# Two pairs of banks for the first batch's row maxima, and later slots for projection, gate and expert choice

## The chip, the cores and the metric

The kernel runs on one core of one Trainium2 chip. The metric is the device time of one execution in microseconds. The engines of the core run side by side, each through its own list of instructions in order, and meet only at semaphores: TensorE (PE, with its weight loads as PEld), VectorE (DVE), ScalarE (ACT), GpSimd (POOL), and SyncE (SP), which issues DMAs.

## The reference, cut to what matters

Eight sequences of 256 token ids go through one block of a language model with width 256:

```python
h = onehot(x) @ embeddings                           # (8, 256, 256)
qkv = layernorm(h) @ w_qkv                           # 16 heads of 16
q, k = rotary(q), rotary(k)
attn = softmax(q @ k.T * 16**-0.5)                   # (8, 16, 256, 256)
h = h + (attn @ v) @ w_proj
y = layernorm(h)
chosen = argmax(y @ gate_w.T)                        # one of 8 experts for each token
h = h + (y + (y @ expert_w[chosen].T))
```

Everything is float32. The kernel splits each float32 operand of a product into a high part that fits TensorE's fast format and a low remainder, and adds up three products (high by high, low by high, high by low), so each projection is three matmuls for each half of the width.

## The kernel before, in words

One batch is one sequence: 256 tokens, two tiles `t` of 128 rows. The work is a pipeline over batches, written out by hand. `step(b)` has 16 slots `s`; in it each engine works on several batches at once. In even slots TensorE does `visit(b, v)` with `v = s // 2`: for two heads it makes the transposed scores T of batch b (`t_scores_tile`, into `t_pair`, two banks of PSUM), which ScalarE turns into probabilities with `exp`, and the scores S of batch b+1 (`scores_tile`, into `s_pair`, two more banks), of which VectorE takes the row maxima with `maximum`. A matmul for S waits until `maximum` has read what its bank held before. The maxima are split into two parts (`max_split`), turned by TensorE into rows (`first_max_transpose` for the first half of batch 0, otherwise `max_transpose`), copied by ScalarE (`max_row`) and written by a DMA into the stack of operands, so that T comes out with its maximum already subtracted.

Beside the visits, tables give each remaining piece of work a slot. `FRONT`, `EARLY`, `TWO` and `FOUR` are for the front of batch k (normalise, transpose x, project q and k, rotate, transpose, project v); batch 2 has the table `TWO`, and the part of its front that is not in the table is written out ahead of step 0. `POST` is for what follows the attention of batch k and is counted from slot 0 of step k+1: `o0`, `o1` (transposes of the outputs), `on`, `o_low`, `proj` (`out_project`), `residual`, `stats`, `g_norm`, `y`, `y_low`, `gate`, `gate_t`, `choose`. The experts of batch b-2 run in step b, one unit of six matmuls in every even slot (`experts`), and VectorE adds each unit, masked by the choice, to `acc` (`select`). Up to step 6 all units write the one bank `e_bank`, so unit n waits until `select` of unit n-1 has read it. The loop `for s in range(SLOTS)` in each engine's `step` fixes in what order the pieces of one slot are issued.

GpSimd adds the two halves of the rotation (`rotated_sum`), takes the inverse square roots, gathers the embedding rows of batch b+4 in slot 1 of step b (two indirect DMAs, `gather`), and in slots 1, 5, 9 and 13 of steps 0 and 1 makes the low parts of the expert weights (`expert_weights`).

Ahead of step 0 stands an opening that is written out: the fronts of batches 0, 1 and in part 2, and the eight visits `visit(-1, v)` that make only S of batch 0. `fill` issues matmuls with a result that nothing reads. `first_restack` on SP moves batch 1's operands by DMA into their stack, and step 0 starts with batch 1's S and batch 0's T.

Of the kernel before, what the change touches and what calls it, by code (L numbers as in the profile page):

```python
# [35 lines left out]
def tower(nc, x, emb, w_qkv, w_proj, gate_w, expert_w, rope, ramp, out):  # L36
# [12 lines left out]
    with ExitStack() as ctx:  # L49
# [76 lines left out]
        def pair_of_banks(name):  # L126
# [47 lines left out]

        FRONT = dict(stats=-8, norm=-6, x=-5, x_low=-4, qk0=-3, qk1=-1, rotate0=-2, rotate1=0, t0=1, low0=2, t1=3, low1=4, v=5)
        EARLY = dict(stats=-12, norm=-9, x=-7, x_low=-6, qk0=-5, qk1=-4, rotate0=-3, rotate1=-2, t0=0, low0=1, t1=2, low1=3, v=5)
        TWO = dict(rotate0=0, rotate1=1, t0=2, low0=3, t1=4, low1=5, v=7)
        FOUR = dict(FRONT, stats=-10, norm=-8, x=-7, x_low=-6, qk0=-5, rotate0=-3, qk1=-2)
        POST = dict(o0=2, o1=4, norm0=3, norm1=5, on=6, o_low=7, proj=8, residual=9, stats=10, g_norm=11,
                    y=12, y_low=13, gate=14, gate_t=15, choose=15)  # L180
        LAST = dict(o0=2, o1=2, norm0=3, norm1=3, on=4, o_low=5, proj=6, residual=7, stats=7, g_norm=8,
                    y=9, y_low=10, gate=11, gate_t=12, choose=12)

# [51 lines left out]

        def maxima_slot(b):

            return 10 if b < 3 else 11

        def place(h):  # L240

# [115 lines left out]
        def _(pool):  # L357
# [19 lines left out]
            def f_rs_of(b):  # L377
# [3 lines left out]
                wait(pool, f_var, b + 1)  # L381
                g.tensor_tensor(f_rs[:, :], f_ve[:, :], neg_half[:, :], ALU.pow).then_inc(f_rstd, 1)

            def rotated_sum(b, t):
                wait(pool, roped, b * 2 * NT + 2 * t + 2)
                if b == 1:
                    pool.wait_ge(z_hi, 2 * t + 2)
                    pool.wait_ge(z_dup_q, t + 1)
                    pool.wait_ge(z_dup_k, t + 1)
                    pool.wait_ge(z_lo, 2 * t + 2)  # L390

                j = 4 if b == 1 else 8
                turned = qk[:, t, :, :, :].rearrange("p g d j -> p (g d j)").rearrange("p (g d j) -> p g j d", d=HD, j=j)
                g.tensor_tensor(turned, rope_a[:, t, :, :].rearrange("p (g j) d -> p g j d", j=j),  # L394
                                rope_b[:, t, :, :].rearrange("p (g j) d -> p g j d", j=j),
                                ALU.add).then_inc(rotated, 1)
# [60 lines left out]
            rotated_sum(1, 0)  # L457
            rotated_sum(1, 1)
            f_rs_of(2)
            gather(3)  # L460
            gate_weights()
            proj_weights_low()
# [4 lines left out]
        def _(pe):  # L467
# [44 lines left out]
            def project_qk(b, t, parts=range(C)):  # L512
                if parts[0] > 0:
                    pass
                elif t == 0:
                    if b == 0:
                        pe.wait_ge(wqkv_l_ok, C)
                    wait(pe, xl_ok, b + 1)
                    if b == 2:
                        wait(pe, qkl_ok, 1)  # L520
                elif b == 2:
                    wait(pe, qkl_ok, 2)
                elif b == 3:
                    wait(pe, qkl_ok, (b - 1) * NT)
                elif b > 3:
                    wait(pe, roped, b * 2 * NT + 2)
                x_h, x_l = x_parts(b)
                m = product(front_bank(b, t)[:, :], lambda c: x_h[:, c, t, :], lambda c: x_l[:, c, t, :],
                            lambda c: wqkv_h[:, c, 0:2 * D], lambda c: wqkv_l[:, c, 0:2 * D], parts)
                if parts[-1] == C - 1:  # L530
                    m.then_inc(qk_ps, 1)
# [33 lines left out]
            def scores_wait(b, v, half):  # L565
                if b == 0 and v == 0:
                    wait(pe, z_in, z_copied(1, 1))
                elif b == 0 and v in (4, 6):
                    wait(pe, z_in, max(z_copied(0, v // 2), z_copied(1, v // 2)))
                elif b == 1 and v % 4 == 0:  # L570
                    wait(pe, half_in[v // 4], 96)
                elif v == 0:
                    wait(pe, stack_in, (b - 2) * 96 + 96)
                wait(pe, max_ok, b * NH + 2 * v - half)

            def scores_tile(b, v, half, t):
                r, pair = place(2 * v + half)
                m = mm(s_pair[:, half, t * N:(t + 1) * N], stacks[b % STACKS][r:r + KS, pair, 0, t * P:(t + 1) * P],  # L578
                       stacks[b % STACKS][r:r + KS, pair, 1, :], start=True, stop=True)
                if t == NT - 1:  # L580
                    m.then_inc(s_ps, 1)

            def first_max_transpose():

                pe.wait_ge(roped, 2 * 2 * NT)
                pe.wait_ge(ml_ok, 1)
                for t in range(NT):
                    m = tr(t_bank[1][0:16, N + t * P:N + (t + 1) * P].bitcast(F32R),
                           max_parts[:, 0, t, :, :, :].rearrange("p i a j -> p (i a j)"), ident_r[:, :])
                m.then_inc(mt_ps, 1)  # L590

# [11 lines left out]
            def t_scores_wait(b, v, half):  # L603
                if v == 0 and b == 1:
                    pe.wait_ge(ones_in, 64)
                if v == 0 and b == 0:
                    pe.wait_ge(wp_l_ok, 1)
                    pe.wait_ge(gw_l_ok, 1)
                    pe.wait_ge(roped, 2 * 2 * NT)
                    pe.wait_ge(filled, VALS + 1)  # L610
                if v % 4 == 0:
                    wait(pe, m_in[v // 4], b * 32 + 32)
                wait(pe, exp_ok, b * NH + 2 * v + half - 1)

            def t_scores_tile(b, v, half, c):
# [108 lines left out]
            def step(b, p):  # L724
                for s in range(SLOTS):
                    g_at = SLOTS * b + s
                    if s % 2 == 0:
                        visit(b, s // 2)
                        if b == 0 and s == 0:
                            project_qk(2, 1, [1])  # L730
                            pe.wait_ge(xl_ok, 3)
                        if b == 0:
                            fill(m_bank, 3 if s == 0 else 4 if s == 2 else 1)
                    if here(b, 0) and s == 3:
                        max_transpose(b, 1)
                    if here(b, 1) and s == maxima_slot(b + 1):
# [53 lines left out]
            z_transpose(1)  # L790
            visit(-1, 0)
            qk_transpose(1, 0)
            visit(-1, 1)
            qk_transpose(1, 1)
            visit(-1, 2)
            x_transpose(2)
            visit(-1, 3)
            project_v(0, [0])
            first_max_transpose()
            visit(-1, 4)  # L800
            project_v(0, [1])
            project_qk(2, 0, [0])
            visit(-1, 5)
            project_v(1, [0])
            project_qk(2, 0, [1])
            visit(-1, 6)
            project_v(1, [1])
            visit(-1, 7)
            project_qk(2, 1, [0])
            steps(step)  # L810


        @block.scalar
        def _(act):
# [35 lines left out]

            def max_row(b, u):
                wait(act, mt_ps, b * 2 + u + 1)
                turned = t_bank[1] if b == 0 and u == 0 else o_bank
                copy(max_rows[:, u, :], turned[0:16, N:2 * N]).then_inc(mt_ok, 1)
                if b == 0 and u == 0:
                    act.wait_ge(mt_ok, 1)
                    for half in range(2):
                        r = 64 * half + KS
                        act.dma_start(stacks[0][r:r + 2, 0:4, 0, :].bitcast(F32),
                                      max_rows[8 * half:8 * half + 8, u, :].bitcast(F32)).then_inc(m_in[u], 16)  # L860
# [77 lines left out]
                z_copy(t, q)  # L938
            qk_high(1, 0)
            qk_high(1, 1)  # L940
            qk_high_again(1, 0)
            qk_high_again(1, 1)
            x_high(2)
            max_row(0, 0)
            values(0)
            values(1)
            steps(step)


# [1 line left out]
        def _(dve):  # L951
# [48 lines left out]
            def maximum(b, k):  # L1000
                for half in (1, 0):
                    wait(dve, s_ps, b * NH + 2 * k + 2 - half)
                    v.tensor_reduce(neg_max[:, k // 4, :, 4 * half + k % 4],  # L1003
                                    s_pair[:, half, :].rearrange("p (t n) -> p t n", t=NT), AX.X, ALU.max,
                                    negate=True).then_inc(max_ok, 1)

            def max_split(b, u):
# [115 lines left out]
            def step(b, p):  # L1123
                for s in range(SLOTS):
# [9 lines left out]
                            g_norm_a(k)  # L1134
                    for k in batches(post, "g_norm", g_at):
                        g_norm_b(k)
                    if here(b, -2) and s > 0 and unit_in(b, s - 1) is not None:
                        select(b - 2, p, unit_in(b, s - 1), expert_banks(b - 2))
                    for k in batches(front, "stats", g_at):
# [19 lines left out]
                            g_norm_a(k)  # L1159
                    for k in batches(post, "y_low", g_at):  # L1160
                        y_low(k, k % 2)
                    for k in batches(post, "choose", g_at):
                        choose(k, k % 2)

            dve.sem_inc(acc_ok, 1)
            for b in range(NB):
                v.memset(h0[:, b * NT:(b + 1) * NT, :], 0.0).then_inc(h_zero, 1)
# [26 lines left out]
                v.memset(vals[i][:, :, :, HD:HD + 1], 1.0).then_inc(filled, 1)  # L1194
            maximum(0, 0)
            f_norm_a(2)
            maximum(0, 1)
            f_norm_b(2)
            qk_low(1, 0)
            maximum(0, 2)  # L1200
            qk_low(1, 1)
            maximum(0, 3)
            max_split(0, 0)
            x_low(2)
# [32 lines left out]
```

## Time and profile before

| | us |
|---|---|
| median of 3 runs | 310.89 (310.54 to 310.95) |
| profiled execution, its own time | 310.0 |
| its span | 308.2 |
| PE busy | 283.4 (92% of the span) |
| DVE busy | 243.4 (79%) |
| ACT busy | 132.7 (43%) |
| POOL busy | 85.9 (28%) |
| mean granted TensorE clock | 0.983 of full |

The span runs from the first to the last instruction, and the execution's own time is 1.8 us more. A busy time is the sum of the records of an engine; matmul records overlap, so a full PE share does not say that the PE does all it could. The page gives the PE 64% of the chain of work that ended last, and DVE 24%.

### The profile page before, as it was taken

To read this page: it belongs to the slowest core of one execution; us is meant where nothing else is said; L and a number is where in the kernel's file an instruction comes from. 1 tells how busy PE (TensorE), PEld (TensorE's weight loads), DVE (VectorE), ACT (ScalarE), POOL (GpSimd) and SP (SyncE) were. 2 spreads that over 40 slices of the span, in tenths; PEclk is the share of its full clock that TensorE was granted. 3 is DMA by queue.
4 is the path that set the end of the run, shared out by engine and by line. 5 is a ranking of instruction groups with operands and counts; after the bars stand their busy time and mean duration, and the time that the engine had idled before them with its cause. 6 is when DMAs were issued, how large, how long until landed. Compare 5 with 4: busy or idle time off the path is not lost.

```text
span 308.2 us, 5639 instructions
## 1 busy us (share of the span) xinstructions
PE 283.4 (92%) x2063; PEld 203.1 (66%) x2063; DVE 243.4 (79%) x602; ACT 132.7 (43%) x271; POOL 85.9 (28%) x103
## 2 busy tenths in 40 slices
PE   2998799888879999999999999999999999999895
PEld 2775566656646776777767776777666666667674
DVE  8798569968987799887988698878898874656765
ACT  3166117748664534364426433453453444331000
POOL 5736305636265012431222033201200210210300
PEclk9999579999999999999999999999999999999999
DMA  4530410830930580039101940166010010000011
GB/s 117 182 149 17 160 45 6 167 49 14 161 47 5 95 120 2 0 93 147 17 2 36 147 60 2 36 116 94 2 37 1 4 36 2 1 12 26 0 36 34
DMA packets 10803, 17.55 MB, mean 57 GB/s; under 512 B 2024, under 2 KB 4883, under 8 KB 10648
## 3 DMA queue, kind: packets, MB, share of 16 engines
q1 hardware_dynamic: 9988, 16.62, 26.2%
q0 software_dynamic: 768, 0.55, 0.7%
q8 instruction: 17, 0.28, 0.4%
q14 instruction: 10, 0.08, 0.1%
q10 hardware_dynamic: 20, 0.02, 0.0%
HBM read 5.30 MB, written 2.10 MB: 24 GB/s over the span
## 4 chain that ended last, share of the span: by engine, by line
PE 64%; DVE 24%; ACT 5%; issue 3%; DMA 1%; POOL 0%; SPq 0%; DVEq 0%; ACTq 0%
PE e_bank L475 18%; PE f_bank L475 10%; PE o_bank L652 9%; DVE neg_max L1003 7%; PE t_pair L617 5%; DVE acc L1101 4%; PE s_pair L475 4%; PE s_pair L578 3%; PE m_bank L475 3%; PE s_pair L481 2%; PE o_bank L475 2%; PE m_bank L666 2%; PE m_bank L698 2%; ACT probs L867 2%; ACT parts L816 1%
## 5 line engine op out<-in xcount | busy, mean ns | idle before, releaser
L867 ACT ACTIVATE probs<-t_pair 128x512 f32<-128x512 f32 x128 | 69.5, 595 | 80.1 <-PE t_pair L617 79.6
L1003 DVE TENSOR_REDUCE neg_max<-s_pair 128x2 f32<-128x512 f32 x128 | 81.9, 682 | 13.0 <-PE s_pair L578 12.8
L578 PE MATMUL s_pair<-stacks 48*128 48x256 f32 x256 | 49.5, 316 | 1.5 <-DVE neg_max L1003 0.8
L617 PEld LDWEIGHTS t_pair<-stacks 50*128 50x128 f32 x256 | 32.8, 186 | 22.7 <-issue 20.8
L617 PE MATMUL t_pair<-stacks 50*128 50x256 f32 x256 | 46.6, 308 | 1.1 <-DVE neg_max L1003 0.6
L475 PE MATMUL e_bank<-ew_h,y_h 128*128 128x512 f32 x92 | 40.3, 438 | 1.9 <-DVE acc L1101 1.5
L1101 DVE SCALAR_TENSOR_TENSOR acc<-e_bank,mask,acc 128x256 f32<-128x256 f32 x66 | 28.8, 478 | 11.8 <-PE e_bank L475 11.7
L578 PEld LDWEIGHTS s_pair<-stacks 48*128 48x128 f32 x256 | 34.3, 190 | 4.5 <-DVE neg_max L1003 3.5
L475 PE MATMUL e_bank<-ew_l,y_h 128*128 128x512 f32 x92 | 36.4, 396 | 0.0
L394 POOL TENSOR_TENSOR qk<-rope_a,rope_b 128x512 f32<-128x512 f32 x16 | 20.8, 1301 | 56.2 <-DVE rope_b L990 56.2
L475 PE MATMUL e_bank<-ew_h,y_l 128*128 128x512 f32 x92 | 36.2, 394 | 0.0
L652 PE MATMUL o_bank<-probs,vals 128*32 128x256 f32 x512 | 34.2, 385 | 0.0
L475 PEld LDWEIGHTS e_bank<-ew_h,y_h 128*128 128x128 f32 x92 | 17.3, 188 | 8.9 <-DVE acc L1101 3.9
L652 PEld LDWEIGHTS o_bank<-probs,vals 128*32 128x32 f32 x512 | 13.4, 109 | 12.2 <-issue 5.0
L400 POOL TENSOR_SCALAR g_ve<-g_mv 128x2 f32<-128x2 f32 x8 | 1.9, 243 | 68.9 <-DVE g_mv L959 68.9
L475 PEld LDWEIGHTS e_bank<-ew_l,y_h 128*128 128x128 f32 x92 | 17.3, 188 | 4.1
L370 POOL DMA_INDIRECT h<-in_emb,ids x16 | 17.6, 1098 | 5.5 <-issue 3.3
L816 ACT ACTIVATE o_t<-o_bank 128x256 f32<-128x256 f32 x32 | 12.5, 389 | 14.7 <-PE o_bank L652 14.7
L475 PEld LDWEIGHTS e_bank<-ew_h,y_l 128*128 128x128 f32 x92 | 17.4, 189 | 2.1
L475 PE MATMUL f_bank<-wqkv_h,x_h 128*128 128x256 f32 (+1 forms) x46 | 16.5, 358 | 1.8 <-DVE x_l L974 1.8
L475 PE MATMUL f_bank<-wqkv_h,x_l 128*128 128x256 f32 (+1 forms) x46 | 15.7, 342 | 0.0
L475 PE MATMUL f_bank<-wqkv_l,x_h 128*128 128x256 f32 (+1 forms) x46 | 15.7, 341 | 0.0
(177 smaller groups left out, 542.5 us busy)
## 6 DMA issues: line engine op xcount, KB each, us to landing
stacks<-parts SPq DMA_DIRECT2D x36, 256.0 KB, 6.7
ew_raw<-in_expert_w SPq DMA_DIRECT2D x1, 2048.0 KB, 8.5
out<-res SPq DMA_DIRECT2D x7, 256.0 KB, 2.1
stacks<-parts SPq DMA_DIRECT2D x12, 128.0 KB, 2.8
probs<-in_w_qkv SPq DMA_DIRECT2D x2, 384.0 KB, 3.8
stacks<-max_rows SPq DMA_DIRECT2D x30, 8.0 KB
h<-in_emb,ids POOLq DMA_INDIRECT x16, 2.7
probs<-in_w_proj SPq DMA_DIRECT2D x1, 256.0 KB, 2.7
```

The lines of the kernel that those rows point to most:

```text
L370: g.indirect_dma_start(h0[:, j, :], None, emb, bass.IndirectOffsetOnAxis(ap=ids[:, j:j + 1], axis=0), bounds_check=V - 1, oob_is_err=False ...
L394: g.tensor_tensor(turned, rope_a[:, t, :, :].rearrange("p (g j) d -> p g j d", j=j), rope_b[:, t, :, :].rearrange("p (g j) d -> p g j d", ...
L475: m = mm(o, a(c), w(c), start=(c == 0 and n == 0), stop=(c == C - 1 and n == 2))
L481: mm(o[:, :], wqkv_h[:, 0, 0:P], wqkv_h[:, 0, 0:512], start=True, stop=True)
L578: m = mm(s_pair[:, half, t * N:(t + 1) * N], stacks[b % STACKS][r:r + KS, pair, 0, t * P:(t + 1) * P], stacks[b % STACKS][r:r + KS, pair, ...
L617: m = mm(t_pair[:, half, c * N:(c + 1) * N], stacks[b % STACKS][r:r + KM, pair, 1, c * P:(c + 1) * P], stacks[b % STACKS][r:r + KM, pair, ...
L652: m = mm(o_bank[STRIP * j:STRIP * (j + 1), 0:N], vals[b % VALS][:, c, head(4 * g + j), :], probs[:, (4 * g + j) % RING, c, :], start=(c == ...
L666: m = tr(strips_bank(b, t)[:, g * P:(g + 1) * P], o_t[:, g, t * P:(t + 1) * P], ident[:, :])
L816: return nc.scalar.activation(o, i, ACT.Copy)
L867: nc.scalar.activation(probs[:, (2 * v + half) % RING, :, :].rearrange("p c n -> p (c n)"), t_pair[:, half, :], ACT.Exp, scale=SCALE).then ...
L1003: v.tensor_reduce(neg_max[:, k // 4, :, 4 * half + k % 4], s_pair[:, half, :].rearrange("p (t n) -> p t n", t=NT), AX.X, ALU.max, negate=T ...
L1101: v.scalar_tensor_tensor(out=acc[:, j, t, :], in0=y, scalar=mask[:, p, t, e:e + 1], in1=base[:, t, :] if u == 0 else acc[:, j, t, :], op0= ...
```

## The change

Batch 0's S visits with odd `v` go to `t_pair`, which batch 0's T does not need yet; their waits on `max_ok` are those of the visit before last, and the first T waits for all 16 maxima. The order of the opening on TensorE, ScalarE and VectorE is rearranged, with five fills in it; the last third of batch 2's projection moves from slot 0 of step 0 into it; and the normalisation of batch 2 goes from VectorE (`f_norm_b(2)`) to GpSimd (`normed(2)`). In `TWO` the rotations of batch 2 go from slots 0 and 1 to 1 and 3, its transposes and low parts one slot later. In `POST`, `proj` goes from slot 8 to 9, `gate` from 14 to 15, `gate_t` from 15 to 16 and `choose` from 15 to 17; `residual` stays at 9. `choose` is now issued ahead of `select` within a slot. `maxima_slot` is 11 for every batch.

```diff
-        TWO = dict(rotate0=0, rotate1=1, t0=2, low0=3, t1=4, low1=5, v=7)
+        TWO = dict(rotate0=1, rotate1=3, t0=3, low0=4, t1=5, low1=6, v=7)
-        POST = dict(o0=2, o1=4, norm0=3, norm1=5, on=6, o_low=7, proj=8, residual=9, stats=10, g_norm=11,
-                    y=12, y_low=13, gate=14, gate_t=15, choose=15)
+        POST = dict(o0=2, o1=4, norm0=3, norm1=5, on=6, o_low=7, proj=9, residual=9, stats=10, g_norm=11,
+                    y=12, y_low=13, gate=15, gate_t=16, choose=17)
...
         def maxima_slot(b):
-            return 10 if b < 3 else 11
+            return 11
+
+        def scores_pair(b, v):
+            return t_pair if b == 0 and v % 2 else s_pair
...
+            def normed(b):
+                pool.wait_ge(f_rstd, b + 1)
+                for t in range(NT):
+                    g.tensor_scalar(xn[:, t, :], h0[:, b * NT + t, :], f_mv[:, t, 0:1], f_rs[:, t:t + 1],
+                                    ALU.subtract, ALU.mult).then_inc(f_normed, 1)
...
             f_rs_of(2)
+            normed(2)
             gather(3)
...
                 elif v == 0:
                     wait(pe, stack_in, (b - 2) * 96 + 96)
-                wait(pe, max_ok, b * NH + 2 * v - half)
+                if b == 0 and v == 1:
+                    pe.wait_ge(roped, 2 * 2 * NT)
+                if b == 0:
+                    wait(pe, max_ok, 2 * v - 2 - half if v > 1 else 0)
+                else:
+                    wait(pe, max_ok, b * NH + 2 * v - half)
...
+                if v == 0 and b == 0:
+                    pe.wait_ge(max_ok, NH)
                 wait(pe, exp_ok, b * NH + 2 * v + half - 1)
...
                         visit(b, s // 2)
-                        if b == 0 and s == 0:
-                            project_qk(2, 1, [1])
-                            pe.wait_ge(xl_ok, 3)
                         if b == 0:
-                            fill(m_bank, 3 if s == 0 else 4 if s == 2 else 1)
+                            fill(m_bank, 3 if s < 4 else 1)
...
             z_transpose(1)
             visit(-1, 0)
             qk_transpose(1, 0)
+            project_v(0, [0])
             visit(-1, 1)
             qk_transpose(1, 1)
+            project_v(0, [1])
             visit(-1, 2)
+            fill(m_bank, 1)
+            project_v(1, [0])
+            visit(-1, 3)
             x_transpose(2)
-            visit(-1, 3)
-            project_v(0, [0])
+            project_v(1, [1])
+            visit(-1, 4)
             first_max_transpose()
-            visit(-1, 4)
-            project_v(0, [1])
             project_qk(2, 0, [0])
             visit(-1, 5)
-            project_v(1, [0])
             project_qk(2, 0, [1])
+            fill(m_bank, 1)
             visit(-1, 6)
-            project_v(1, [1])
+            project_qk(2, 1, [0])
+            fill(m_bank, 1)
             visit(-1, 7)
-            project_qk(2, 1, [0])
+            project_qk(2, 1, [1])
+            fill(m_bank, 2)
             steps(step)
...
             qk_high(1, 0)
             qk_high(1, 1)
+            values(0)
             qk_high_again(1, 0)
             qk_high_again(1, 1)
             x_high(2)
+            values(1)
             max_row(0, 0)
-            values(0)
-            values(1)
...
             maximum(0, 0)
             f_norm_a(2)
+            qk_low(1, 0)
             maximum(0, 1)
-            f_norm_b(2)
-            qk_low(1, 0)
+            qk_low(1, 1)
             maximum(0, 2)
-            qk_low(1, 1)
             maximum(0, 3)
```

Left out of the diff are `first_max_transpose` and `max_row`, which use `e_bank` in place of a bank of `t_pair` for batch 0's first turn, with the waits that belong to it, and VectorE's `maximum`, which reads `scores_pair(b, k)`.

## Rows read from the trace of the kernel before

**Rows 1.** The page: the granted clock of TensorE in 40 slices.

```profile
PEclk9999579999999999999999999999999999999999
```

**Rows 2.** Windows: the opening and steps 0, 3 and 5; busy us, clock, DMA share.

```profile
25.40:46.10 20.70, 17.52 (x79) 12.18 (x79) 13.85 (x29) 6.12 (x12) 5.78 (x7) 0.75 0.25 82
46.10:68.70 22.60, 20.68 (x169) 13.85 (x169) 19.26 (x37) 14.96 (x30) 11.20 (x11) 1.00 0.42 75
...
127.50:160.50 33.00, 32.18 (x251) 23.50 (x250) 28.30 (x74) 14.69 (x31) 9.35 (x11) 1.00 0.35 61
...
193.50:222.70 29.20, 28.52 (x235) 20.89 (x234) 23.62 (x55) 14.35 (x30) 4.92 (x6) 1.00 0.37 65
```

**Rows 3.** Windows of one us of PE alone: length, PE busy, clock, DMA share, GB/s.

```profile
31.00:32.00 1.00, 0.58 (x3) 0.93 0.63 186
...
42.00:43.00 1.00, 1.00 (x7) 0.95 0.00 0
```

**Rows 4.** Timeline of PE, the first fills: start, us, instruction.

```profile
5.71 5.84 PE L481 MATMUL s_pair<-wqkv_h 128*128 128x512 f32 x13 [5.71 <-ACT wqkv_h L816]
...
11.74 1.41 PE L481 MATMUL s_pair<-wqkv_h 128*128 128x512 f32 x5
```

**Rows 5.** Timeline of DVE, the opening and step 0.

```profile
25.99 1.29 DVE L1003 TENSOR_REDUCE neg_max<-s_pair 128x2 f32<-128x512 f32 x2 [0.52 <-PE s_pair L578]
...
28.07 1.26 DVE L1003 TENSOR_REDUCE neg_max<-s_pair 128x2 f32<-128x512 f32 x2
...
29.99 0.67 DVE L995 TENSOR_TENSOR parts<-f_bank,parts 128x512 fp32r<-128x512 f32 x1
...
56.35 1.18 DVE L1010 CAST max_parts<-neg_max 128x16 fp32r<-128x16 f32 x1
```

**Rows 6.** Chain of waits, opening and step 1: start, us, engine, tile, line, count.

```profile
22.51 1.46 PE t_pair L475 x6
...
25.45 0.56 PE s_pair L578 x4
...
38.38 1.65 PE f_bank L475 x3
...
75.80 1.43 PE f_bank L475 x12
```

**Rows 7.** Timeline of ACT, the last copy ahead of `project_v(0, [0])`.

```profile
26.71 0.65 ACT L816 ACTIVATE stacks<-o_bank 128x512 fp32r<-128x512 f32 x1
```

**Rows 8.** Timeline of POOL in step 0.

```profile
50.18 1.29 POOL L394 TENSOR_TENSOR qk<-rope_a,rope_b 128x512 f32<-128x512 f32 x1 [1.08 <-DVE rope_b L990]
51.61 1.02 POOL L370 DMA_INDIRECT h<-in_emb,ids  x1
52.93 1.00 POOL L370 DMA_INDIRECT h<-in_emb,ids  x1 [0.30 <-issue]
53.96 1.29 POOL L417 TENSOR_TENSOR ew_l<-ew_raw,ew_h 128x512 fp32r<-128x512 f32 x1
55.21 0.22 POOL L380 TENSOR_SCALAR f_ve<-f_mv 128x2 f32<-128x2 f32 x1
```

**Rows 9.** Chain of waits in step 3.

```profile
139.09 1.00 PE o_bank L652 x16
...
147.09 0.67 DVE h L1033 x2
...
151.54 0.48 DVE acc L1101
...
152.06 1.66 PE e_bank L475 x6
```

**Rows 10.** Timeline of PE: waits in step 1, in step 2 and near the end.

```profile
91.69 0.29 PE L698 MATMUL m_bank<-y_h,gw_parts 128*16 128x256 f32 x1 [0.70 <-DVE y_l L1048]
...
96.62 0.66 PE L545 MATMUL f_bank<-ident,qk 128*128 128x128 f32 x4 [0.38 <-DVE rope_b L990]
...
293.22 0.29 PE L706 MATMUL m_bank<-ident,gate_rows 16*128 16x16 f32 x2 [0.46 <-ACT gate_rows L816]
```

More of the change, by code:

```diff
@@ L521, in project_qk @@
                 elif b == 2:
-                    wait(pe, qkl_ok, 2)
+                    wait(pe, mt_ok, 1)
                 elif b == 3:
@@ L573, in scores_wait @@
                     wait(pe, stack_in, (b - 2) * 96 + 96)
-                wait(pe, max_ok, b * NH + 2 * v - half)
+                if b == 0 and v == 1:
[4 more added lines that the diff above has]
+                    wait(pe, max_ok, b * NH + 2 * v - half)
             def scores_tile(b, v, half, t):
                 r, pair = place(2 * v + half)
-                m = mm(s_pair[:, half, t * N:(t + 1) * N], stacks[b % STACKS][r:r + KS, pair, 0, t * P:(t + 1) * P],
+                m = mm(scores_pair(b, v)[:, half, t * N:(t + 1) * N], stacks[b % STACKS][r:r + KS, pair, 0, t * P:(t + 1) * P],
                        stacks[b % STACKS][r:r + KS, pair, 1, :], start=True, stop=True)
@@ L583, in first_max_transpose @@
             def first_max_transpose():
-                pe.wait_ge(roped, 2 * 2 * NT)
+                pe.wait_ge(qkl_ok, NT)
                 pe.wait_ge(ml_ok, 1)
                 for t in range(NT):
-                    m = tr(t_bank[1][0:16, N + t * P:N + (t + 1) * P].bitcast(F32R),
+                    m = tr(e_bank[0:16, N + t * P:N + (t + 1) * P].bitcast(F32R),
                            max_parts[:, 0, t, :, :, :].rearrange("p i a j -> p (i a j)"), ident_r[:, :])
@@ L852, in max_row @@
                 wait(act, mt_ps, b * 2 + u + 1)
-                turned = t_bank[1] if b == 0 and u == 0 else o_bank
+                turned = e_bank if b == 0 and u == 0 else o_bank
                 copy(max_rows[:, u, :], turned[0:16, N:2 * N]).then_inc(mt_ok, 1)
@@ L1003, in maximum @@
                     v.tensor_reduce(neg_max[:, k // 4, :, 4 * half + k % 4],
-                                    s_pair[:, half, :].rearrange("p (t n) -> p t n", t=NT), AX.X, ALU.max,
+                                    scores_pair(b, k)[:, half, :].rearrange("p (t n) -> p t n", t=NT), AX.X, ALU.max,
                                     negate=True).then_inc(max_ok, 1)
@@ L1136, in step @@
                         g_norm_b(k)
+                    for k in batches(post, "choose", g_at):
+                        choose(k, k % 2)
                     if here(b, -2) and s > 0 and unit_in(b, s - 1) is not None:
@@ L1161, in step @@
                         y_low(k, k % 2)
-                    for k in batches(post, "choose", g_at):
-                        choose(k, k % 2)
             dve.sem_inc(acc_ok, 1)
```

## The prediction

> **What bounds the kernel now.** I read the slices of the page first: the granted clock is full everywhere except in slices 4 to 6 [rows 1]. The windows by step then show three regimes. The opening from the first visit takes 20.7 us at a mean clock of 0.75 [rows 2], and windows of one us bound its slow stretch: the clock falls just before 32 and is back just after 42, so 10.2 us at 1.2 GHz in place of 2.4 [rows 3]. Ahead of the fall the PE had thin work: visits, transposes, and waits for `maximum`, 0.58 busy in the last microsecond. In step 0 both PE and DVE are nearly full. In steps 3 and 5 the PE is busy for 32.2 of 33.0 and 28.5 of 29.2 us [rows 2]: what delays the PE there is paid in full. The chain of step 3 shows where DVE holds it: from the residual of `proj` at 147.09 DVE works almost without a pause to a `select` that ends at 152.02, and the next expert unit starts at 152.06 [rows 9].
>
> **The opening.** Four facts give the new one. (a) Prices at full clock: six 512-column matmuls 1.46, so 0.73 for three; six 256-column ones 0.72, half of twelve at 1.43; an S visit 0.5 to its next neighbour, 0.56 to the maximum [rows 6]; a fill 0.28 with its tail, 0.24 in a row [rows 4]. At half clock three 512-column ones took 1.65 [rows 6]. (b) `project_v(0, [0])` waits for ScalarE's last stack copy, until 27.36 [rows 7]. (c) DVE takes 1.2 from one maximum to the next start, 0.88 for the statistics (27.19 to 28.07), 0.6 for a low part [rows 5]. (d) A visit no longer waits for the maximum directly before it.
>
> I put TensorE's new list in order with these: products of v from 27.4, visit 1 at 28.2, transposes, products, visit 2 at 30.0, a fill, products, visit 3 at 31.55, x transposes, products, visit 4 at 33.35, then the turn of the maxima (it waits for DVE's split, done at 33.55) and four groups of three 512-column matmuls with visits 5, 6, 7 between, the last visit at 38.1. DVE reads the last maxima from 38.55 to 39.8. Step 0 starts at 39.9 in place of 46.1: **minus 6.2**. DVE alone would allow 38.7; if the clock fell again as before, the PE list at half price gives 43.9. I take 39.9, because the PE is idle for only 1.0 us (26.4 to 27.4) and then issues without a gap, unlike before the old fall. The DMAs of `first_restack` were issued after the low parts; these end earlier now, so the data should be there.
>
> POOL's `normed(2)` is not in the trace. The nearest rows are 1.29 for two 512-wide inputs and 0.22 for two columns [rows 8]; so 0.4 to 2.6 for both halves, I take 1.5. It is done at 30.8, the x transposes want it at 32.05; only the upper end reaches them. It also moves `gather(3)` and POOL's low projection weights 1.5 later, close to DVE's `max_split`. The trace shows what such a meeting costs: the cast of 56.35 took 1.18 [rows 5] while POOL made expert weights, so 1.0 lost. I price it at zero with 1.0 as its upper end. The Trainium skill ("SBUF — State Buffer", section "SBUF: two separate sides") says why and would make it order-dependent: whichever of a two-input or fast-mode VectorE operation and a GpSimd operation starts first holds their shared port for the whole instruction. By that page the opening loses 1.0 only if POOL comes first, and the sum would be 1.0 higher.
>
> **Step 0, the queue of POOL.** This is the part that goes wrong. Times from the start of the step: the visit, DVE's first maximum from 0.57 to 1.8, then `rotate(2, 0)`, two operations of 0.6, to 3.05 (before, it ran ahead of the maximum). POOL's sum takes 1.29, so `qk_transpose(2, 0)` is issued at 4.5. The PE has by 3.1 done visit 1, three fills and the turn, and waits 1.4. The second half is worse. In slot 1 of POOL `gather(4)` and `expert_weights([0])` stand behind `rotated_sum(2, 0)`, and `rotated_sum(2, 1)` is now in slot 3, behind them. In the trace both sums came first; from the end of the second, at 51.47, two gathers and one weight part went until 55.21, 3.74 us [rows 8]. So the second sum runs from 4.42 + 3.74 = 8.17 to 9.46, and `qk_transpose(2, 1)`, its outputs and all that follow wait until 9.5, after visit 2 has ended at about 5.8: 3.7 us of idle PE. From there I count transposes 0.45, outputs 1.0, visit and fill 0.9, `project_v(2)` 1.45, visit and fill 0.9, x transposes 0.45, outputs 1.0: visit 5 at 15.65. Before, it stood at 13.96, with 1.0 of that the cast above. **Plus 1.7.** Bounds: minus 1.0 (POOL not in the way) and plus 2.7 (the cast held again). From visit 5 on the order is the old one: `maxima_slot` 10 or 11 has the same neighbours on every engine in steps 0 and 1, so this edit is nothing.
>
> **Step 0, the clock.** Between 3.1 and 9.5 the PE has 1.35 us of work in 6.4. That is thinner than the stretch ahead of the fall of 32. I expect a fall. How long it lasts has two precedents: from the first fill at 5.71 thirteen fills took 0.45 each, the next five, from 11.74, 0.28 [rows 4], so 5.7 to 6 us of dense work ran slow; the other lasted 10.2 [rows 3]. Slow work loses half of its time. I take the 5.7, since here too dense work follows an idle stretch: 2.85, less 0.5 that hides in waits for ScalarE. **Plus 2.3**, bounds 0 and 4.6.
>
> **Step 1.** The wait of 0.70 for `y_l` goes, as three 512-column products now stand ahead of `gate`; and `choose` no longer stands ahead of the rotation, so the 0.38 at 96.62 goes [rows 10]. `out_project` behind the outputs makes `residual`, x's low part and the next projection later, about 0.4. **Minus 0.7**, bounds minus 1.1 and plus 0.5.
>
> **Steps 2 to 6.** `out_project` goes behind `outputs(b, 1)`, which takes 1.0 on the PE [rows 9]. `residual` stays in its slot and DVE is in order, so behind it wait statistics, x's norm, the fifth maximum, y's norm and `select(5)`. In step 3 the product ended at 146.8 and DVE took it at once; it will end at 147.8, and DVE stands from 147.01 to 147.82. The 5.0 us behind it are full, so the next expert unit starts at 152.87 in place of 152.06: 0.81. The outputs that the PE does earlier free nobody, since ScalarE copies them only after the next visit's exponentials. Nothing in the rest of the step gives it back: PE is full. In steps 5 and 6 DVE has 0.5 us of slack ahead of the residual, but is then later by a full 1.0, and 0.8 reaches the PE. Five steps, **plus 4.1**; bounds 0 and 5. Moving `gate` and `gate_t` trades places among PE work of equal sum. `choose`, about 1 us, goes behind a maximum and ahead of `select(0)`, which ends at 164.5 in place of 164.0 in step 3, and the unit that needs it starts at 164.89: hidden, with 0.4 to spare.
>
> **The end.** From step 7 to 8 no visit stands between `gate` and `gate_t`; ScalarE's copy between them showed 0.46 of waiting once [rows 10]. **Plus 0.4**, bounds 0 and 0.5.
>
> **Sum.** -6.2 + 1.7 + 2.3 - 0.7 + 4.1 + 0.4 = +1.6. The profiled execution, 310.0, becomes 311.6; the median stood 0.9 above it, so 312.5.
>
> **The rivals.** (1) *The late residual does not reach the PE*: DVE catches up in steps 2 to 6, and then 4.1 falls away: 308.4, faster than before. It decides once the loss is below 0.5 a step. For it: DVE is busy only 28.3 of 33.0 us. Against it: its idle time lies elsewhere, and the chain is tight. (2) *The clock holds in step 0*: minus 2.3, 310.2. For it: windows of the old step 1 with waits of 1.2 us kept full clock. Against it: 3.7 us idle at a stretch. (3) Both: 306.1. (4) *The fall in step 0 lasts as long as the old one*: 10.2 us, plus 2.3, 314.8. (5) *The opening still falls to half clock*, step 0 starts at 43.9: plus 4.0, 316.5, and the second pair of banks has done little of what it is for.
>
> **Chances.** Forecast 0.45, with its own range 311.0 to 314.0; (1) 0.13; (2) 0.17; (3) 0.05; (4) 0.12; (5) 0.08. The range 308.2 to 315.2 leaves out (3), (5) and half of (1). Within 0.2% means 310.27 to 311.51, about what a measurement can tell. Faster takes (1), (3), over half of (2) and a tail of the forecast: 0.33. Same, 0.15: the rest of (2) and 0.08 of the forecast. Slower 0.52.
>
> **What would show it.** Right: step 0's first T at 39 to 40.5 and full clock until then; the second sum of POOL in step 0 after two gathers and a weight part, the PE idle some 3.7 us ahead of `qk_transpose(2, 1)`, and a clock below 1 behind it; steps 3 and 4 of 33.8 us, with DVE waiting about 0.8 for the PE ahead of `h`. Wrong: steps of 33.0, a clock that never falls, or a start of step 0 past 42.

## The result, and the profile after

The changed kernel takes 318.21 us (median of 4, 316.81 to 319.40) against 310.72 for the kernel before on the same chips: ratio 1.0241, 95% interval 1.0189 to 1.0294. It is slower, as forecast, but by 7.5 us and not 1.6; the time lies outside the range. The profiled execution took 317.29, with a span of 315.5.

Step lengths say where. A step starts with its first T matmul; the opening is what comes before step 0, the end is everything from the start of step 7. Microseconds of the two profiled executions:

| | opening | step 0 | 1 | 2 | 3 | 4 | 5 | 6 | end | span |
|---|---|---|---|---|---|---|---|---|---|---|
| before | 46.13 | 22.59 | 25.18 | 33.61 | 33.01 | 33.00 | 29.24 | 27.02 | 58.42 | 308.2 |
| after | 40.84 | 27.04 | 25.77 | 34.62 | 34.08 | 33.91 | 30.50 | 28.56 | 60.18 | 315.5 |
| measured change | -5.29 | +4.45 | +0.59 | +1.01 | +1.07 | +0.91 | +1.26 | +1.54 | +1.76 | +7.3 |
| forecast | -6.2 | +4.0 | -0.7 | +0.8 | +0.8 | +0.8 | +0.8 | +0.8 | +0.4 | +1.6 |

The page's clock, by slices, as in [rows 1]: the slow slices of the opening are gone, and one has come in step 0 (the dip in slice 6).

```profile
PEclk9999995999999999999999999999999999999999
```

POOL in step 0, the answer to [rows 8] (start, us, instruction). The second `qk` sum stands behind two gathers and a weight part:

```profile
43.94 1.28 POOL L404 TENSOR_TENSOR qk<-rope_a,rope_b 128x512 f32<-128x512 f32 x1 [8.10 <-DVE rope_b L1010]
45.37 1.02 POOL L374 DMA_INDIRECT h<-in_emb,ids  x1
46.69 1.00 POOL L374 DMA_INDIRECT h<-in_emb,ids  x1 [0.30 <-issue]
47.71 1.28 POOL L427 TENSOR_TENSOR ew_l<-ew_raw,ew_h 128x512 fp32r<-128x512 f32 x1
48.94 1.27 POOL L404 TENSOR_TENSOR qk<-rope_a,rope_b 128x512 f32<-128x512 f32 x1
```

What the PE makes of it, in its timeline; the bracket is the idle time and who ended it:

```profile
45.37 0.63 PE L556 MATMUL f_bank<-ident,qk 128*128 128x128 f32 x4 [1.01 <-POOL qk L404]
50.36 1.08 PE L556 MATMUL e_bank<-ident,qk 128*128 128x128 f32 x4 [3.26 <-POOL qk L404]
```

The same four transposes take 0.63 before the stall and 1.08 after it. Windows of the PE (length, busy, clock, DMA share, GB/s) show that the clock fell while it stood, as [rows 3] show it for the old opening, and came back near 55.4: 6.8 us, of which the PE worked 5.0.

```profile
46.00:48.00 2.00, 1.10 (x9) 1.00 0.10 27
48.00:50.00 2.00, 0.00 (x0) 0.65 0.06 19
50.00:52.00 2.00, 1.64 (x12) 0.50 0.03 8
...
54.00:56.00 2.00, 2.00 (x14) 0.64 1.01 197
56.00:58.00 2.00, 2.00 (x19) 1.00 0.42 91
```

The chain of step 3, the answer to [rows 9]: unit 4 is followed by the outputs, then `out_project`, then DVE's residual, and the next unit that waits.

```profile
144.85 1.66 PE e_bank L486 x6
146.51 1.00 PE o_bank L670 x16
147.51 1.62 PE m_bank L486 x12
...
149.16 0.77 DVE h L1053 x2
...
153.69 0.49 DVE acc L1121
...
154.22 1.67 PE e_bank L486 x6
```

The length from the residual to unit 6 is 5.06 us, as before (147.09 to 152.06, 4.97). The timeline of DVE has what stands ahead of it, a wait that the old step 3 did not have:

```profile
149.16 0.76 DVE L1053 TENSOR_TENSOR h<-m_bank,h 128x256 f32<-128x256 f32 x2 [0.93 <-PE m_bank L486]
```

Two waits of the PE that the forecast had not priced, in step 2 and in step 7, and the DVE wait that the second goes back to:

```profile
98.79 0.51 PE L486 MATMUL e_bank<-ew_h,y_h 128*128 128x512 f32 x1 [0.50 <-DVE acc L1117]
...
275.51 0.66 PE L708 MATMUL m_bank<-ident,yn 128*128 128x128 f32 x4 [1.26 <-DVE yn L1063]
```

```profile
271.82 0.76 DVE L1053 TENSOR_TENSOR h<-m_bank,h 128x256 f32<-128x256 f32 x2 [3.05 <-PE m_bank L486]
```

A third thing stands in the rows of step 6 and was not foreseen. `choose` no longer stands ahead of `max_split`, so DVE comes to the split sooner, while POOL makes the sum for the output. POOL started first, and the second half of the split took 0.72, until POOL was done; the kernel before had 0.17 for it there, behind `choose`.

```profile
227.36 0.73 POOL L421 TENSOR_TENSOR res<-acc 128x256 f32<-128x256 f32 x1 [2.52 <-DVE acc L1121]
```

```profile
227.39 0.72 DVE L1032 TENSOR_TENSOR max_parts<-neg_max,max_parts 128x16 fp32r<-128x16 f32 x1
```

The same comes again in step 7, and at the start of step 2 with a weight part: there the cast took 0.82 and not 0.17.

### The profile page after: what moved, and what is told of

Read it like the earlier page. It is cut to its first block, busy times and chain, and to the rows that moved or that the text cites. A ratio compares the mean times of both kernels' runs of the same rounds, so it can differ in the third digit from the quotient of the medians.

```text
span 315.5 us, 5649 instructions
## 1 busy us (share of the span) xinstructions
PE 284.3 (90%) x2067; PEld 201.8 (64%) x2067; DVE 245.2 (78%) x600; ACT 134.7 (43%) x271; POOL 88.4 (28%) x105
## 4 chain that ended last, share of the span: by engine, by line
PE 59%; DVE 23%; issue 7%; POOL 4%; ACT 4%; DMA 1%; SPq 0%; DVEq 0%; POOLq 0%
PE e_bank L486 18%; PE o_bank L670 9%; PE f_bank L486 9%; DVE neg_max L1023 5%; PE s_pair L486 4%; PE m_bank L486 4%; DVE acc L1121 4%; PE t_pair L635 4%; PE s_pair L492 2%; DVE h L1053 2%; DVE g_st L976 2%; PE m_bank L684 2%; POOL h L374 1%; PE m_bank L692 1%; PE s_pair L594 1%
## 5 line engine op out<-in xcount | busy, mean ns | idle before, releaser
L1023 DVE TENSOR_REDUCE neg_max<-s_pair 128x2 f32<-128x512 f32 x120 | 77.0, 684 | 12.7 <-PE s_pair L594 12.6
L635 PE MATMUL t_pair<-stacks 50*128 50x256 f32 x256 | 47.8, 311 | 1.8 <-DVE neg_max L1023 0.6
L594 PE MATMUL s_pair<-stacks 48*128 48x256 f32 x240 | 46.0, 312 | 0.1
L670 PE MATMUL o_bank<-probs,vals 128*32 128x256 f32 x512 | 35.1, 393 | 0.0
L594 PEld LDWEIGHTS s_pair<-stacks 48*128 48x128 f32 x240 | 31.9, 187 | 0.9 <-issue 0.4
L1053 DVE TENSOR_TENSOR h<-m_bank,h 128x256 f32<-128x256 f32 x16 | 6.0, 419 | 12.3 <-PE m_bank L486 12.3
```

The lines of the kernel that those rows point to most:

```text
L594: m = mm(scores_pair(b, v)[:, half, t * N:(t + 1) * N], stacks[b % STACKS][r:r + KS, pair, 0, t * P:(t + 1) * P], stacks[b % STACKS][r:r + ...
L635: m = mm(t_pair[:, half, c * N:(c + 1) * N], stacks[b % STACKS][r:r + KM, pair, 1, c * P:(c + 1) * P], stacks[b % STACKS][r:r + KM, pair, ...
L670: m = mm(o_bank[STRIP * j:STRIP * (j + 1), 0:N], vals[b % VALS][:, c, head(4 * g + j), :], probs[:, (4 * g + j) % RING, c, :], start=(c == ...
L1023: v.tensor_reduce(neg_max[:, k // 4, :, 4 * half + k % 4], scores_pair(b, k)[:, half, :].rearrange("p (t n) -> p t n", t=NT), AX.X, ALU.ma ...
L1053: v.tensor_tensor(h1[:, t, :], m_bank[:, t * D:(t + 1) * D], h0[:, b * NT + t, :], ALU.add).then_inc(h1_ok, 1)
```

## The experiments

Each ran on one chip with the kernel before (310.3 to 310.4 there); ratios are to it. Step lengths are those of the one profiled execution. "Clock" is the mean granted clock of an execution; 1.000 means that it never fell.

**1. proj alone.** On the kernel before:

```diff
-        ... on=6, o_low=7, proj=8, residual=9, ...
+        ... on=6, o_low=7, proj=9, residual=9, ...
```

> The kernel before with proj in slot 9 in place of 8, nothing else. Theory (the late residual is the largest loss): the steps with proj grew by 0.9 to 1.5 us in the changed kernel, 1.03 of it from visit 4 to the sixth expert unit in step 3. In step 1 and in step 7 it costs about 1.3 each, in steps 2 to 6 about 1.0 each: 7.6 us in all, so 318.5 against 310.9. DVE waits 0.9 for the PE ahead of the residual in step 3 and 3.0 in step 7. Rival (the 0.81 of the prediction is right and the rest of the growth comes from gate and choose): plus 4.1, 315.0.

Measured: 320.61 us, ratio 1.0301 (1.0244 to 1.0357). One number in a table makes the kernel slower than the whole change does. Steps 2 to 6 take 34.61, 34.01, 34.05, 30.41 and 28.23: 1.0, 1.0, 1.05, 1.2 and 1.2 more, as expected and not 0.8. The end takes 59.27, plus 0.85 (1.3 expected). The opening is 0.9 longer too, with a longer stretch of slow clock. Step 1 takes 29.09, plus 3.9 against an expected 1.3: the PE waits 1.39 for x's norm, and the clock falls within that wait. Windows of step 1:

```profile
82.00:84.00 2.00, 0.72 (x4) 0.64 1.05 153
84.00:86.00 2.00, 2.00 (x18) 0.50 1.05 155
```

The four executions had clocks from 0.963 to 0.984 and times from 321.4 to 317.8: how long the clock is low differs from one execution to the next. Where it fell is known for the profiled one alone; of the fastest, a mean of 0.984 leaves about 10 us at half clock (an estimate from its span of 315.9), no more than the old opening had.

**2. gate, gate_t and choose alone.** On the kernel before:

```diff
-                    y=12, y_low=13, gate=14, gate_t=15, choose=15)
+                    y=12, y_low=13, gate=15, gate_t=16, choose=17)
```

with `choose` issued ahead of `select`.

> The kernel before with gate in slot 15, gate_t in 16, choose in 17 and ahead of select. Theory: step 1 minus 0.7, step 2 plus 0.5 (the second expert unit waits for a select behind choose), steps 3 to 5 nothing, step 6 plus 0.4, the end plus 0.5: plus 0.7, 311.6. Rival (the gate moves carry the growth of steps 2 to 6 that proj does not explain): plus 3 or more, 314.

Measured: 309.76 us (10 executions), ratio 1.0003 (0.9976 to 1.003). Step 1 takes 24.45 (minus 0.73, for the forecast's wait of 0.70), step 2 32.98 (minus 0.63; plus 0.5 was expected), steps 3 and 4 minus 0.1 each, 5 nothing, 6 plus 0.3, the end plus 1.0. So the gates gain early and lose late, and carry none of the growth of steps 2 to 5. The 0.50 of waiting in step 2 of the changed kernel is theirs: it stands here too, and not in experiment 1. The expectation was right about that wait and missed that others of about 0.4 in the same step go.

**3. Fills in the gap of step 0.** On the changed kernel:

```diff
-                            fill(m_bank, 3 if s < 4 else 1)
+                            fill(m_bank, 3 if s == 0 else 8 if s == 2 else 15 if s == 4 else 1)
```

> The changed kernel with 20 fills more in step 0, 5 ahead of the transpose of batch 2's first tile and 14 ahead of the second, where the PE stands idle for GpSimd. Theory (the idle stretch drops the clock, and the slow stretch behind it costs about 2.5 us): the clock stays full in step 0, the wait stays, and the four executions of the changed kernel that lay between 316.8 and 319.4 come together near 315.3. Rival (the slow clock hides behind VectorE and ScalarE): the clock is full and the time stays at 317 to 318.

Measured: two executions at 315.36 and 315.47 (clock 0.994) and two at 319.2 (0.984); median 317.34, ratio 1.0205 (1.0138 to 1.0272). The edit adds 19 fills. In the profiled one, of the slower two, the clock of step 0 is full and the step takes 24.84 in place of 27.04, while the second sum of POOL is as late as before. So the slow clock cost 2.2 us there, the forecast's 2.3, and it does not hide; the rest of the growth of step 0, 2.25, is the queue of POOL and what goes with it. That the executions would come together was wrong: here the clock fell in the opening, which no profiled execution of it had shown so far, and twice in step 1.

```profile
26.00:28.00 2.00, 1.19 (x7) 0.88 0.09 25
28.00:30.00 2.00, 2.00 (x11) 0.50 0.00 0
30.00:32.00 2.00, 2.00 (x14) 0.76 0.00 0
```

**4. The gather later.** On the changed kernel, POOL's `step`:

```diff
-                    if s == 1 and here(b, 4):
+                    if s == (4 if b == 0 else 1) and here(b, 4):
                         gather(b + 4)
-                    if s % 4 == 1 and b < 2:
-                        expert_weights([4 * b + s // 4])
+                    if s % 4 == 1 and b < 2 and g_at > 1:
+                        expert_weights([4 * b + s // 4] if g_at > 5 else [0, 1])
```

> The changed kernel with GpSimd's gather of batch 4 in slot 4 of step 0 in place of slot 1 and the first expert weight part in slot 5, so that nothing stands between the two sums of batch 2's rotation. Theory: the second sum starts at 46.3 in place of 48.9, the PE waits 0.5 and not 3.3 us ahead of that transpose, and the clock does not fall: minus 2.7 for the wait and minus 2.5 for the clock, about 313.0. Rival (the late rotation on VectorE holds the second transpose whatever GpSimd does): under 1 us, 317.

Measured: 315.57 us, ratio 1.0192 (1.0146 to 1.0239): 5.2 above the kernel before, where the changed kernel was 7.5 above it. The second sum starts at 46.03; the PE waits 0.68 and not 3.26:

```profile
47.47 1.09 PE L556 MATMUL e_bank<-ident,qk 128*128 128x128 f32 x4 [0.68 <-POOL qk L404]
```

Step 0 goes from 27.04 to 24.21, with a shorter stretch of slow clock as a part of that. The queue of POOL is shown. The clock part of the expectation failed: it fell all the same after waits of only 1.00 and 0.68, and again in step 1, so 313.0 was not reached.

**5. proj back.** The changed kernel with `proj=8`.

> The changed kernel with proj back in slot 8. Theory: steps 1 to 7 lose 5.5 us of growth in steps 2 to 6 and about 1.3 each in step 1 and at the end, and step 1 no longer lets the clock fall in some executions; what stays is the gain of the opening (5.3) against step 0 (4.5): 310.2, within 0.5 of the kernel before. Rival (proj and the gates together cost more than apart, so that proj back alone gives only the 5.5): 312.5 or more.

Measured: 309.61 us (10 executions, 308.55 to 312.0), ratio 0.9973 (0.994 to 1.0006). Steps 2 to 5 take 33.60, 32.98, 32.86 and 29.32, within 0.15 of the kernel before. Against the kernel before on the same chip the time goes from 7.5 above to 0.7 below: 8.2 us hang on this one number, more than the whole loss.

**6. The opening alone.** The changed kernel with `TWO` and `POST` of the kernel before, and `choose` behind the other work of its slot again.

> The changed kernel's opening with everything behind it as before: TWO, proj, gate, gate_t and choose in their old slots, choose behind the other work of its slot. maxima_slot stays 11. Theory: step 0 starts at 40.8 in place of 46.1 and then takes its old 22.6 us less 0.2, with full clock throughout, and maxima_slot is worth nothing: 305.0. Rival (step 0 pays the opening back whatever the slots are, because VectorE or the DMAs of the restack are late): 309 or more.

Measured: 304.17 us (303.94 to 304.33), ratio 0.9787 (0.9743 to 0.9832). Step 0 starts at 40.80 and takes 22.11; the later steps stand within 0.1 of the kernel before. Three of the four executions had a clock of 1.000. The page of it:

```profile
PEclk9999999999999999999999999999999999999999
```

**7. The opening, and the gates for four batches.** As 6, with the new slots of `gate`, `gate_t` and `choose` for batches 0 to 3, and `choose` ahead of `select` for all batches:

```diff
-            return SLOTS * (k + 1) + (LAST if last(k) else POST)[what]
+            later = {'gate': 1, 'gate_t': 1, 'choose': 2}.get(what, 0) if k < 4 else 0
+            return SLOTS * (k + 1) + (LAST if last(k) else POST)[what] + later
```

> As e6_opening_alone, and the new slots of gate, gate_t and choose for batches 0 to 3 only, with choose ahead of select for all. Theory: steps 1 to 4 keep what the gate moves gave alone (0.7, 0.6, 0.1, 0.1) and steps 6 to 8 do not pay for them: 303.5, the fastest so far. Rival (with an earlier step 1 the gate moves give nothing): 305.

Measured: 305.27 us, ratio 0.9842 (0.9787 to 0.9896); 1.1 slower than 6. Step 1 gained its 0.74, but step 6 takes 28.24 in place of 27.03, and the end 0.6 more. The rows name the cause: `choose` of batch 4, in its old slot, stands ahead of the last `select` now and waits for the turned gate, so the first unit of step 6 waits too.

```profile
218.00 0.50 PE L487 MATMUL e_bank<-ew_h,y_h 128*128 128x512 f32 x1 [1.28 <-DVE acc L1122]
```

The same wait, 0.50 long, stands at the start of step 7.

**8. The opening with one pair of banks.** As 6, but:

```diff
-            return t_pair if b == 0 and v % 2 else s_pair
+            return s_pair
```

and the old wait on `max_ok`.

> As e6_opening_alone, but all S visits of batch 0 in s_pair again, each waiting for the maximum before it; the order of the opening, its fills and GpSimd's norm stay. Theory (the gain comes mostly from the order and the full clock, the second pair gives the rest): step 0 starts at 42 to 42.5, 306.3. Rival (the second pair is what keeps the PE from waiting and the clock up): the PE waits before every visit, the clock falls, step 0 starts at 44 to 46, 308.5 to 310.

Measured: 305.17 us, in two pairs: 304.23 and 304.29 with a clock of 1.000, 306.05 and 306.13 with 0.994 and a fall in step 1; ratio 0.981 (0.9756 to 0.9864). Step 0 starts at 41.19 and not at 40.80: the second pair of banks is worth 0.4 us of the 5.3. The rest lies in what this run kept: the new order, the fills and the norm on POOL. The products of v stand between the visits from the first one on, the PE waits 0.81 at most and DVE 0.58, and the clock stays up. These three were not tried one by one, so how much of it the fills give is open.

**9. proj late, x's norm in the gap.** As 1, but batch 6's `proj` in slot 8, and:

```diff
-        FRONT = dict(stats=-8, norm=-6, ...
+        FRONT = dict(stats=-8, norm=-7, ...
```

> As e1_proj_alone (proj in slot 9), with two differences: batch 6's proj stays in slot 8, and the table FRONT has norm at -7 in place of -6, so that in steps 2, 3 and 4 VectorE normalises x while it would stand and wait for the product, and not behind it. Theory (VectorE's chain behind the late residual is what the PE waits for): steps 2 to 4 lose about 0.6 of the 1.0 to 1.05 us that they had gained and take 33.4 us in place of 34.0 (step 2: 34.0); steps 5 and 6, where there is no x to normalise, stay at 30.4 and 28.2; the last part from step 7 on goes back from 59.3 to 58.4. Rival (the PE pays by itself, through weight loads or the place of the outputs): steps 2 to 4 stay at 34.0.

Measured: 315.46 us, ratio 1.0181 (1.0149 to 1.0214). Step 1, where the clock holds this time with the same wait of 1.40 for x's norm, takes 26.48: the late `proj` alone costs 1.3 there. Steps 3 and 4 take 33.41 and 33.42 in place of 34.01 and 34.05, step 2 34.06 in place of 34.61; steps 5 and 6 stay at 30.43 and 28.22; the end is back at 58.39. DVE's timeline in step 3 has the norm (`xn`) ahead of the residual (`h`), whose wait shrinks from 0.92 in experiment 1 to 0.28:

```profile
148.61 0.86 DVE L1101 SCALAR_TENSOR_TENSOR acc<-e_bank,mask,acc 128x256 f32<-128x256 f32 x2
149.40 0.73 DVE L968 TENSOR_SCALAR xn<-h,f_mv,f_rs 128x256 f32<-128x256 f32 x2
150.40 0.75 DVE L1033 TENSOR_TENSOR h<-m_bank,h 128x256 f32<-128x256 f32 x2 [0.28 <-PE m_bank L475]
```

0.6 us taken off DVE's chain is 0.6 us off the step. The PE alone cannot be the cause, since nothing was changed on it in these steps. The 0.4 that stay were not taken apart.

**10. The gates for four, choose in its place.** As 7, with `choose` ahead of `select` only for batches 0 to 3.

> As e7_opening_and_gates, but choose is issued ahead of select only for batches 0 to 3, whose choose is in the new slot, and behind the other work of its slot for the others. Theory (in step 6 of e7 choose stood ahead of the last select in slot 15 and made the next expert unit wait): step 6 goes from 28.2 back to 26.8, step 1 stays at 24.4, 302.9, faster than the opening alone. Rival (the time of step 6 comes from the gate slots of batch 3): 305 as before.

Measured: 302.72 us (7 executions, 302.45 to 304.53), ratio 0.9749 (0.9734 to 0.9765). Step 6 is back at 27.04 as expected, and the end at 58.4. Step 2 takes 32.96, where 7 had 33.60 and a wait of 0.54 for `o_n`, though nothing was changed there: why is open. In the two executions above 304 the clock was 0.992. The profiled one is of these: step 1 takes 25.98, and the clock falls at 75.6, just behind a wait of 0.65 for the low part of the outputs. `proj` stands in its old slot here, as in experiment 8, whose clock fell at the same place of step 1. So a fall in step 1 does not need the late `proj`.

**11. Fills in the waits.** As 10, with fills in three places:

```diff
                     if here(b, 1) and s == maxima_slot(b + 1):
+                        if b == 1:
+                            fill(e_bank, 4)
                         max_transpose(b + 1, 0)
...
+                            if k == 0:
+                                fill(e_bank, 3)
                             out_project(k)
...
             qk_transpose(1, 0)
+            pe.wait_ge(roped, 2 * 2 * NT)
+            fill(t_bank[0], 4)
             project_v(0, [0])
```

> As e9_gates_for_four, with 4 fills where the opening waits for ScalarE's last stack copy, 3 ahead of batch 0's projection in step 1 and 4 where step 1 waits for ScalarE's copy of the outputs. Theory (thin stretches there let the clock fall in some executions): median within 0.3 of e9, no execution below a clock of 0.999, no execution more than 0.5 above the fastest. Rival (the fills delay the work behind them): 0.5 or more slower than e9.

Measured: 302.66 us (5 executions, 302.45 to 302.86), ratio 0.9752 (0.9737 to 0.9767). Step 1 takes 24.45 with full clock, and the lowest mean clock of the five is 0.999, too high for a fall like that of experiment 10. It is the fastest version along with 10, 7.6 us below the kernel before, with a spread of 0.4 where 10 had 2.1. That the fills hold the clock is not shown by this: 10 had five executions of seven near 302.5 without them, and experiment 6 four of four at 304, so five in a row can be chance. What is shown is that the fills cost nothing.

## Why the prediction was wrong

The direction and the mechanisms of the largest terms were right, the sum was not: the five parts were each too kind, by 5.7 us together. The largest miss is the term for steps 2 to 6. In step 1, in step 6 and at the end a wait had been left out.

- **The opening** (forecast -6.2, measured -5.29). The order and the full clock came as forecast, and the wait for the stack copies was 0.8 in place of 1.0. Visit 4 stood at 33.36, the forecast's 33.35. From there the PE list was priced too low: the last visit came at 38.65 and not 38.1, since the turn of the maxima ended 0.2 late and three groups, two visits and two fills took 4.02, where the forecast's prices give 3.67. Behind it DVE read the last maximum until 40.48 and not 39.8, and step 0 started at 40.84, not 39.9. POOL's norm took 2.44 and not 1.5, and still came in time. The forecast did not price the second pair of banks by itself; experiment 8 says that it gives 0.4.
- **The queue of POOL** (+1.7) had the right mechanism: 3.7 us of idle PE forecast, 3.26 in the bracket, with the second sum 5.0 us behind the first one's start, as worked out. Experiment 4 takes it away. Its size was 2.25, step 0 at full clock in experiment 3 against the old 22.59. The meeting with POOL that the price of 1.0 stood for did not happen in the opening: the two halves of the split took 0.18 and 0.28, ahead of the weight part at 34.56. So in the opening the rule of the Trainium skill ("SBUF — State Buffer", section "SBUF: two separate sides"), by which a POOL operation that comes first would block VectorE, was not put to the test. In step 6 it was, and the trace agrees: POOL's sum started at 227.36 and took 0.73, the split started at 227.39 and took 0.72.
- **The clock in step 0** (+2.3) was right: 2.2 by experiment 3. Some of that is luck, as the slow stretch was longer than the 5.7 forecast, 6.8, but with 1.8 of idle time in it.
- **Step 1** (-0.7, measured +0.59 where the clock held). The wait of 0.70 for `y_l` went, and experiment 2 gives 0.73 for it. The 0.38 at 96.62, which the forecast counted here, lies in step 2; it went too, and the new wait of 0.50 came close behind it. The step that failed is "`out_project` behind the outputs makes ... about 0.4": x's transposes stand between them and wait 1.40 for DVE, which normalises x only after the low part of the outputs; visit 5 came 0.85 later, visit 6 1.3. The late `proj` alone costs 1.3 at full clock (experiment 9), the gates give 0.73 back. Besides, the clock fell in step 1 in the profiled executions of experiments 1, 3, 4, 8 and 10, with the late `proj` and without. The forecast weighed a fall of the clock only in step 0 and in the opening. The two executions of the changed kernel at 319 had mean clocks of 0.978 and 0.982, against 0.988 of the two at 317; where theirs fell no trace shows.
- **Steps 2 to 6** (+4.1, measured +5.8). The step "the next expert unit starts ... 0.81" later had the right mechanism, shown by experiments 1, 5 and 9. Its size was 1.0 in steps 2 to 4 and 1.2 in 5 and 6 (experiment 1): `out_project` takes 1.62 behind the outputs where it took 1.4 behind an expert unit, so in step 3 the residual waited 0.93. In step 6 a further 0.3 comes from the gates, by experiment 2 (step 6 plus 0.3): the second unit waits 0.35 for a `select`. `choose` was costed at nothing, because one step had 0.4 us to spare. That cover was read in one step and used for five; in step 6 the unit is due 0.3 sooner after the start of the step, and the split that `choose` used to stand ahead of meets POOL and takes 0.55 more. How the two share the 0.3 was not tried.
- **The end** (+0.4, measured +1.76). The 0.46 for `gate_t` came, and the gates cost 1.0 in all there (experiment 2), with the same meeting of the split and POOL as in step 6. What failed besides is that step 7 was taken for one in which the late residual costs nothing; it costs 0.85 (experiment 1). There the expert units stand in odd slots, so `proj` in slot 9 falls behind a unit as well, the residual waited 3.05 and the transposes of y 1.26.

Of the rivals, the one that was faster than before (the late residual does not reach the PE) is refuted; so is a clock that holds in step 0. That the fall lasts as long as the old one is not what came (6.8 us, not 10.2), and the opening kept its clock in this trace, though not in that of experiment 3.

## What to carry to other kernels

Where a step is moved by one slot, write down everything that each in-order engine now has ahead of it in every variant of the loop (first, last and shortened passes), not in a typical one: here the queue of POOL, the late residual in step 7 and x's transposes in step 1 cost 4.4 us at full clock, next to 5.8 in steps 2 to 6. A product whose consumer sits at the head of another engine's full chain must not be made later, even past work that is free to wait; the delay is then paid in every pass that has such a chain. And where a time jumps between executions by 2 us, look at the granted clock of each first. A few fills in waits of about 1 us cost nothing here; whether they hold the clock takes more executions than these to tell.

## What the runs showed that was not expected

- The clock can fall after far less than the idle 3.26 us of step 0: around two waits of 1.00 and 0.68 us in a thin part of step 0 (experiment 4), behind a wait of 0.65 in step 1 (experiment 10), and in the new opening behind a single wait of 0.81 (experiment 3), where all other profiled executions of that opening held it.
- Whether it falls differs between executions of one kernel: 308.55 to 312.0 in experiment 5, with clocks from 0.994 down to 0.983.
- Two normalisations of 128x256 took POOL 2.44 us, where DVE took 0.78 for the same ones; POOL's sums of two 128x256 inputs took 0.74 each.
- Twelve 256-column matmuls took 1.62 us behind the outputs with their 32-column weights, and 1.4 behind an expert unit. Why was not tried.
